# Three layer normalizations whose scaling moves from VectorE to ScalarE, with additions and small matmuls in another order

## The chip, the cores and the metric

One core of one Trainium2 chip runs the whole program in one launch. The metric is the device time of that launch in microseconds (us), median of three runs. The core has five engines with instruction queues of their own: TensorE (PE in the profile, its weight loads PEld), VectorE (DVE), ScalarE (ACT), GpSimd (POOL) and SyncE (SP), which issues the DMAs. They meet only at semaphores.

## The reference

A chain of four blocks over x of shape (2, 1024, 128) in float32, each with a layer normalization in front and a residual addition behind:

```
x = x + attention(norm(x))      # 16 heads of 8, decay by distance
x = x + experts160(norm(x))     # 160 experts of 64, top 8 by sigmoid scores, one shared expert
x = x + memory(norm(x))         # fast-weight memory, chunks of 64 tokens, one after the other
x = x + experts8(norm(x))       # 8 experts of 256, top 2 within groups
norm(x) = (x - mean(x)) / sqrt(var(x) + 1e-5)      # over the 128 features
```

## The kernel before

The 2048 tokens are 16 tiles of 128 tokens on the partitions, in four groups of four tiles (`G` = 4, `TPG` = 4); one group is 512 columns, `GW`, one bank of PSUM. `x` and `xn` hold tokens by features, `xnT` holds features by tokens. The program is written by hand, engine by engine: the order on each engine is the order of its code, and `wait_ge` on counting semaphores ties the engines together. No scheduler moves anything. Each `norm(k)` stands on four engines, k being 0 to 3 for the four blocks:

- VectorE (L1674): for each group `make_x(g)`, the residual addition, then four `bn_stats` (L1686) and four `bn_aggr` (L1689) into `mv` (mean and variance), which raise `var_ready`; one group later four `tensor_scalar` (L1698), (x - mean) * rstd into `xn`, which raise `xn_ready`.
- GpSimd (L680): variance + EPS (L685), then the power -0.5 (L686) into `rstd`, which raises `rstd_ready`.
- TensorE (L1165): four transposes of `xn` into bank 0 or 1 (L1175), which raise `xnT_psum`; then, one group behind, `read_group`, the first products that read `xnT`. For k = 3 four spare matmuls a group (`spares`, L1172) stand ahead of the transposes of groups 1 to 3; their results are written over. Spare matmuls stand elsewhere too (`spare`, L1185); they compute nothing.
- ScalarE (L869): copies the bank into `xnT` (L874), which raises `xnT_ready`, then, one group behind, `follow`.

Around the three later ones:

- `norm(1)` stands behind the attention. `make_x` is the addition of the projection (L1792). `read_group` is `tokens_of`: the shared expert's product (L1307), four router products into PSUM (L1292), and the biases of a later group (L1286). `follow` is `take_group`: two copies for the shared expert (L1015, L1016), the sigmoid of the scores (L1009) and xh, the rounded high part of `xnT` (L882). VectorE then picks the top eight per token, and the chosen weights go through DRAM into the expert loop (L1464, L1471, L1477 on TensorE).
- `norm(2)` stands behind that loop. `make_x` adds the experts' sum (L1957), `read_group` is `token_scalars` (two spares, then L1533), `follow` is `token_gates`, a sigmoid (L887) whose function table has to be loaded first. Behind it come 32 products for half sums (L1523) and the memory's 16 steps. GpSimd has memsets and casts (L832 to L836) ahead of its part and the inverse norms (L842 to L845) behind.
- `norm(3)` stands behind the memory. Four additions of the memory's output (L2046) come first, then all the statistics. 18 spares (L1593) fill TensorE's time. `read_group` is `router_logits2`: four products of eight columns (L1589). `follow` is `high_x`, xh again (L882); GpSimd makes the low part xl (L856). Behind it the first gate and up products of the second expert stage (L1464 by the helper `three`) take xh and xl, while VectorE chooses experts from the logits (L2058 to L2094).

Of the kernel before, what the change touches and what calls it, by code (L numbers as in the profile page):

```python
# [26 lines left out]
P = 128  # L27
# [57 lines left out]
def build(nc, a, out):  # L85
    with ExitStack() as ctx:
# [26 lines left out]
        ident = sb("ident", [P, P])  # L113
        half = sb("half", [P, NT])
# [542 lines left out]
        def _(pool):  # L657
# [22 lines left out]
            def norm(k):  # L680

                for g in range(G):
                    ts = slice(g * TPG, (g + 1) * TPG)
                    pool.wait_ge(var_ready, G * k + g + 1)
                    link(pool.tensor_scalar(rstd[:, ts], mv[:, ts, 1], EPS, None, ALU.add))  # L685
                    pool.tensor_tensor(rstd[:, ts], rstd[:, ts], half[:, ts], ALU.pow).then_inc(rstd_ready, 1)  # L686
# [172 lines left out]
        def _(act):  # L859
# [9 lines left out]
            def norm(k, follow):  # L869
                for g in range(G):  # L870
                    n = G * k + g
                    act.wait_ge(xnT_psum, n + 1)
                    cols = slice(g * GW, (g + 1) * GW)
                    act.activation(xnT[:, cols], bank(n % 2), ACT.Copy).then_inc(xnT_ready, 1)  # L874
                    if g:
                        follow(g - 1)
# [285 lines left out]
        def _(pe):  # L1162
            pe.wait_ge(consts, 1)

            def norm(k, read_group=None, spares=0):  # L1165

                for g in range(G):
                    n = G * k + g
                    if g >= 2:
                        pe.wait_ge(xnT_ready, n - 1)  # L1170
                    for _ in range(spares if g else 0):
                        pe.matmul(bank(n % 2), hh[0][:, 0:P], hh[0][:], start=True, stop=True)  # L1172
                    pe.wait_ge(xn_ready, n + 1)
                    for t in range(TPG):
                        ins = pe.transpose(bank(n % 2)[:, t * P:(t + 1) * P], xn[:, g * TPG + t, :], ident[:])  # L1175
                    ins.then_inc(xnT_psum, 1)
                    if read_group and g:
                        read_group(g - 1)
                if read_group:
                    read_group(G - 1)  # L1180
# [413 lines left out]
            norm(3, router_logits2, 4)  # L1594
# [76 lines left out]
        def _(dve):  # L1671
            link = Link(dve, dve_link)

            def norm(k, make_x=None):  # L1674

                for g in range(G + 1):
# [17 lines left out]
                    if g >= 1:  # L1694
                        tiles = range((g - 1) * TPG, g * TPG)
                        dve.wait_ge(rstd_ready, G * k + g)
# [346 lines left out]
            for g in range(G):  # L2043
# [5 lines left out]

            norm(3)  # L2050
# [114 lines left out]
```

## Time and profile before

| what | us |
|---|---|
| median of three runs | 1058.62 |
| lowest and highest of them | 1057.59, 1058.99 |
| the profiled execution, its own time | 1059.15 |
| its span in the trace | 1057.4 |
| TensorE busy | 1008.4 (95%) |
| VectorE busy | 816.8 (77%) |
| ScalarE busy | 795.7 (75%) |
| GpSimd busy | 233.0 (22%) |

The span runs from the first to the last instruction in the trace, and the time of the run has a little more around it. Busy TensorE includes the spare matmuls. The mean granted clock of TensorE over the span is 0.987 of full speed.

### The profile page before, as it was taken

Reading aid. Unit: us, or ns where it says so; the run is one execution under the profiler, and the core shown is the slowest. Engines: PE = TensorE matmul, PEld = TensorE weight load, DVE = VectorE, ACT = ScalarE, POOL = GpSimd, SP = SyncE. Lnnn points to the kernel's source line nnn. Section 1 sums busy time; section 2 is a strip of 40 time slices with the busy share of each in tenths; the row PEclk is TensorE's granted clock in tenths of the full one; section 3 lists DMA queues with packets and bytes.
Section 4 is the critical chain, followed back from the end, with each engine's and each line's share of the span. In section 5 each row is a group of like instructions: output and inputs, shape, how many; then the busy total and the mean of one; then the engine's idle time right before and its main releaser. Section 6 shows DMA issues by size and latency. Waiting matters only on the chain.

```text
span 1057.4 us, 20303 instructions
## 1 busy us (share of the span) xinstructions
PE 1008.4 (95%) x5242; PEld 684.2 (65%) x5274; DVE 816.8 (77%) x1861; ACT 795.7 (75%) x1331; POOL 233.0 (22%) x359
## 2 busy tenths in 40 slices
PE   5799999999998999999999999999998998999997
PEld 3333333333335688888888888888875887888885
DVE  8644444444449799999999999999996888699997
ACT  5799999999985778788787878778773553655554
POOL 3777765554463000000000000000005112200000
PEclk9799999999999999999999999999999999899999
DMA  4477876777761587677776777777631000034321
GB/s 134 143 230 242 255 250 219 235 225 226 225 202 36 180 309 246 240 243 235 240 241 241 246 245 236 235 245 242 237 98 60 1 2 1 1 128 125 106 102 40
DMA packets 102991, 188.98 MB, mean 179 GB/s; under 512 B 11932, under 2 KB 56604, under 8 KB 102940
## 3 DMA queue, kind: packets, MB, share of 16 engines
q1 hardware_dynamic: 102756, 188.19, 54.8%
q8 instruction: 18, 0.29, 0.1%
q10 hardware_dynamic: 192, 0.30, 0.1%
q14 instruction: 25, 0.20, 0.1%
HBM read 152.46 MB, written 35.98 MB: 178 GB/s over the span
## 4 chain that ended last, share of the span: by engine, by line
PE 86%; DVE 5%; ACT 3%; DMA 2%; issue 2%; POOL 1%; SPq 1%; DVEq 0%; ACTq 0%; POOLq 0%
PE bank L1464 28%; PE bank L1477 16%; PE bank L1362 12%; PE bank L1471 8%; PE bank L1343 6%; PE bank L1346 5%; PE bank L1562 1%; PE bank L1373 1%; DVE xn L1698 1%; PE bank L1185 1%; DVE stats L1686 1%; DVE state L2036 1%; DMA c_rows<-fold 1%; PE bank L1572 1%; PE bank L1292 1%
## 5 line engine op out<-in xcount | busy, mean ns | idle before, releaser
L1464 PE MATMUL bank<-xh,w_parts 128*128 128x512 f32 x896 | 277.4, 391 | 0.9 <-DVEq L1936 0.9
L969 ACT ACTIVATE ring<-bank,minus_bound 128x1024 f32<-128x1024 f32 x256 | 263.0, 1118 | 13.8 <-PE bank L1346 8.8
L1069 ACT ACTIVATE bank<-bank 128x512 f32<-128x512 f32 x320 | 186.2, 582 | 88.7 <-PE bank L1464 88.7
L1950 DVE TENSOR_TENSOR bank<-bank,ring 128x512 f32<-128x512 f32 x320 | 223.8, 699 | 25.2 <-DMA ring<-c_rows 2.8
L1477 PE MATMUL bank<-hh,w_parts 128*128 128x512 f32 x772 | 237.9, 389 | 0.0
L1942 DVE TENSOR_TENSOR hl<-bank,hh 128x512 fp32r<-128x512 f32 x321 | 218.4, 680 | 0.1
L1842 DVE TENSOR_TENSOR bank<-bank,corner 128x128 f32<-128x128 f32 x256 | 76.4, 298 | 154.3 <-PE bank L1346 151.2
L1464 PEld LDWEIGHTS bank<-xh,w_parts 128*128 128x128 f32 x896 | 168.0, 189 | 37.5 <-DVEq L1936 1.7
L1063 ACT ACTIVATE hh<-bank 128x512 fp32r<-128x512 f32 x321 | 190.4, 593 | 0.8 <-DVE bank L1950 0.5
L1464 PE MATMUL bank<-xl,w_parts 128*128 128x512 f32 x448 | 174.8, 390 | 0.0
L1477 PEld LDWEIGHTS bank<-hh,w_parts 128*128 128x128 f32 x772 | 144.8, 188 | 30.6 <-ACT hh L1063 0.8
L1471 PE MATMUL bank<-hl,w_parts 128*128 128x512 f32 x387 | 151.8, 392 | 2.5 <-DVE hl L1942 2.3
L1362 PE MATMUL bank<-ring,v_cur 128*32 128x512 f32 x1024 | 137.6, 610 | 0.1
L1343 PEld LDWEIGHTS bank<-q_stack,k_stack 128*128 128x128 bf16 x320 | 30.5, 98 | 115.8 <-ACT ring L969 96.3
L832 POOL MEMSET q_stack<- 128x512 f32 x2 | 1.0, 530 | 466.2 <-PE bank L1471 466.2
L1343 PE MATMUL bank<-q_stack,k_stack 128*128 128x384 bf16 (+2 forms) x320 | 97.7, 322 | 1.8 <-issue 0.2
L1346 PE MATMUL bank<-q_stack,k_stack 128*128 128x512 bf16 (+3 forms) x352 | 94.0, 327 | 4.2 <-DMA k_stack<-k_parts 4.2
L1464 PEld LDWEIGHTS bank<-xl,w_parts 128*128 128x128 f32 x448 | 84.4, 188 | 17.8
L1471 PEld LDWEIGHTS bank<-hl,w_parts 128*128 128x128 f32 x387 | 72.6, 188 | 22.3 <-DVE hl L1942 6.1
L1146 ACT ACTIVATE q_stack<-bank 128x512 f32<-128x512 f32 x58 | 34.7, 598 | 51.7 <-PE bank L1464 49.8
L2111 DVE TENSOR_TENSOR q_stack<-big,ring 128x512 f32<-128x512 f32 x64 | 44.3, 693 | 11.4 <-ACTq L1126 3.0
L1362 PEld LDWEIGHTS bank<-ring,v_cur 128*32 128x32 f32 x1024 | 20.2, 108 | 48.6 <-ACT ring L969 39.9
(320 smaller groups left out, 1137.7 us busy)
## 6 DMA issues: line engine op xcount, KB each, us to landing
ring<-c_rows SPq DMA_DIRECT2D x173, 512.0 KB, 4.7
w_parts<-w_pairs SPq DMA_DIRECT2D x160, 128.0 KB, 2.9
w_pairs<-xh SPq DMA_DIRECT2D x16, 768.0 KB, 4.3
q_stack<-q_parts SPq DMA_DIRECT2D x63, 144.0 KB
k_stack<-k_parts SPq DMA_DIRECT2D x189, 48.0 KB
w_pairs<-xl SPq DMA_DIRECT2D x16, 512.0 KB, 3.0
big<-in_w_exp SPq DMA_DIRECT2D x16, 384.0 KB, 4.8
w_ffn_parts<-xl SPq DMA_DIRECT2D x16, 384.0 KB, 3.7
```

The source lines that it names most:

```text
L969: act.activation(ring[:, c % RING * S:(c % RING + 1) * S], wide[(m + c) % SB][:], ACT.Exp, bias=minus_bound[:]).then_inc(exp_done, 1)
L1063: act.activation(hh[(c - 1) % 2][:], hidden, ACT.Copy).then_inc(split, 1)
L1069: act.activation(bank(4 + c % ZB), bank(4 + c % ZB), ACT.Silu).then_inc(silu_ready, 1)
L1343: ins = pe.matmul(wide[(m + c) % SB][:, lo:mid], k_stack[0][u][:, keys], q_stack[1][u][:, lo:mid], start=True, stop=True)
L1346: ins = pe.matmul(wide[(m + c) % SB][:, mid:hi], k_stack[1][u][:, keys], q_stack[0][u][:, mid:hi], start=True, stop=True)
L1362: ins = pe.matmul(bank(6 + u)[at:at + 32, :], v_cur[u][:, done_step % QT, :], ring[:, at_ring + h * 512:at_ring + (h + 1) * 512], start=(d ...
L1464: ins = pe.matmul(out_, w[i], x_[j], start=start and k == 0, stop=stop and k == 2, skip_group_check=not start)
L1471: return pe.matmul(bank(done_step % G), w[0], hl[done_step % 2][:], start=False, stop=False, skip_group_check=True)
L1477: ins = pe.matmul(bank(done_step % G), part, hh[done_step % 2][:], start=opens and k == 0, stop=False, skip_group_check=True)
L1842: dve.tensor_tensor(tile, tile, corner[:], ALU.mult).then_inc(corner_done, 1)
L1942: dve.tensor_tensor(hl[(c - 1) % 2][:], hidden, hh[(c - 1) % 2][:].bitcast(F32), ALU.subtract).then_inc(split, 1)
L1950: dve.tensor_tensor(bank(4 + c % ZB), bank(4 + c % ZB), cb[u][:, g * GW:(g + 1) * GW], ALU.mult).then_inc(hid_ready, 1)
```

## The change

Normalization 0 stays as it is. In 1, 2 and 3:

- VectorE no longer scales; its `norm` ends with the statistics of the last group.
- GpSimd makes a second column per tile, `shift` = -mean * rstd: a negation of the mean ahead of the addition of EPS, a product behind the power. `rstd_ready` is raised behind the product.
- ScalarE makes `xn` = rstd * x + shift, four activations of 128x128 a group with the function Identity and both columns as operands. In its queue xn of group g stands ahead of the copy of xnT of group g-1, and `follow` of group g-2 behind that.

In 3 alone the addition of the memory's output stands ahead of the statistics of its own group instead of all four ahead, the logits of a group stand behind its own transposes instead of behind the next group's, and two spares a group (in bank 7, groups 0 to 3) stand between the two, where there were four ahead of the transposes of groups 1 to 3.

```diff
@@ GpSimd
+                    if k:
+                        link.sign(pool.tensor_scalar(shift[:, ts], mv[:, ts, 0], -1.0, None, ALU.mult))
                     link(pool.tensor_scalar(rstd[:, ts], mv[:, ts, 1], EPS, None, ALU.add))
-                    pool.tensor_tensor(rstd[:, ts], rstd[:, ts], half[:, ts], ALU.pow).then_inc(rstd_ready, 1)
+                    ins = pool.tensor_tensor(rstd[:, ts], rstd[:, ts], half[:, ts], ALU.pow)
+                    if k:
+                        link(ins)
+                        ins = pool.tensor_tensor(shift[:, ts], shift[:, ts], rstd[:, ts], ALU.mult)
+                    ins.then_inc(rstd_ready, 1)
@@ ScalarE
             def norm(k, follow):
-                for g in range(G):
-                    n = G * k + g
-                    act.wait_ge(xnT_psum, n + 1)
-                    cols = slice(g * GW, (g + 1) * GW)
-                    act.activation(xnT[:, cols], bank(n % 2), ACT.Copy).then_inc(xnT_ready, 1)
-                    if g:
-                        follow(g - 1)
+                for g in range(G + 1):
+                    if g < G:
+                        act.wait_ge(rstd_ready, G * k + g + 1)
+                        for t in range(g * TPG, (g + 1) * TPG):
+                            ins = act.activation(xn[:, t, :], x[:, t, :], ACT.Identity, bias=shift[:, t:t + 1], scale=rstd[:, t:t + 1])
+                        ins.then_inc(xn_ready, 1)
+                    if g >= 1:
+                        n = G * k + g - 1
+                        act.wait_ge(xnT_psum, n + 1)
+                        cols = slice((g - 1) * GW, g * GW)
+                        act.activation(xnT[:, cols], bank(n % 2), ACT.Copy).then_inc(xnT_ready, 1)
+                    if g >= 2:
+                        follow(g - 2)
@@ TensorE
-                    for _ in range(spares if g else 0):
-                        pe.matmul(bank(n % 2), hh[0][:, 0:P], hh[0][:], start=True, stop=True)
                     pe.wait_ge(xn_ready, n + 1)
...
-                    if read_group and g:
+                    if spares:
+                        for _ in range(spares):
+                            pe.matmul(bank(7), hh[0][:, 0:P], hh[0][:], start=True, stop=True)
+                        read_group(g)
+                    elif read_group and g:
                         read_group(g - 1)
-                if read_group:
+                if read_group and not spares:
                     read_group(G - 1)
...
-            norm(3, router_logits2, 4)
+            norm(3, router_logits2, 2)
@@ VectorE
-                for g in range(G + 1):
+                for g in range(G if k else G + 1):
...
-                    if g >= 1:
+                    if g >= 1 and k == 0:
                         tiles = range((g - 1) * TPG, g * TPG)
-                        dve.wait_ge(rstd_ready, G * k + g)
+                        dve.wait_ge(rstd_ready, g)
...
-            for g in range(G):
+            def add_memory(g):
...
-            norm(3)
+            norm(3, add_memory)
```

ScalarE in normalization 2, from the last copies of the expert stage on. `xnT` is the transposed input, `big` the rows of token scalars. Before:

```order
L1081 ACTIVATE state<-bank 128x128 x2
L874 ACTIVATE xnT<-bank 128x512 x2
L887 ACT_TABLE_LOAD
L887 ACTIVATE big<-bank,b_pair 2x512
L874 ACTIVATE xnT<-bank 128x512
L887 ACTIVATE big<-bank,b_pair 2x512
L874 ACTIVATE xnT<-bank 128x512
L887 ACTIVATE big<-bank,b_pair 2x512 x2
```

And of the change:

```order
L1094 ACTIVATE state<-bank 128x128 x2
L881 ACTIVATE xn<-x,shift,rstd 128x128 x8
L887 ACTIVATE xnT<-bank 128x512
L881 ACTIVATE xn<-x,shift,rstd 128x128 x4
L887 ACTIVATE xnT<-bank 128x512
L900 ACT_TABLE_LOAD
L900 ACTIVATE big<-bank,b_pair 2x512
L881 ACTIVATE xn<-x,shift,rstd 128x128 x4
L887 ACTIVATE xnT<-bank 128x512
L900 ACTIVATE big<-bank,b_pair 2x512
L887 ACTIVATE xnT<-bank 128x512
L900 ACTIVATE big<-bank,b_pair 2x512 x2
```

Two groups of scaling stand ahead of the first copy of xnT, the third ahead of the second copy, and the fourth behind the table load and the first sigmoid.

TensorE in normalization 3, from the 18 spares to the first gate product; `hh` are the spares, `w_gate` the logits. Before:

```order
L1185 MATMUL bank<-xh 128x512 x18
L1175 MATMUL bank<-ident,xn 128x128 x4
L1172 MATMUL bank<-hh 128x512 x4
L1175 MATMUL bank<-ident,xn 128x128 x4
L1589 MATMUL bank<-w_gate,xnT 128x8 x4
L1172 MATMUL bank<-hh 128x512 x4
L1175 MATMUL bank<-ident,xn 128x128 x4
L1589 MATMUL bank<-w_gate,xnT 128x8 x4
L1172 MATMUL bank<-hh 128x512 x4
L1175 MATMUL bank<-ident,xn 128x128 x4
L1589 MATMUL bank<-w_gate,xnT 128x8 x8
L1464 MATMUL bank<-xh,w_parts 128x512 x2
```

And of the change, the first two of four equal groups and what follows the fourth's transposes:

```order
L1200 MATMUL bank<-xh 128x512 x18
L1186 MATMUL bank<-ident,xn 128x128 x4
L1190 MATMUL bank<-hh 128x512 x2
L1604 MATMUL bank<-w_gate,xnT 128x8 x4
L1186 MATMUL bank<-ident,xn 128x128 x4
L1190 MATMUL bank<-hh 128x512 x2
L1604 MATMUL bank<-w_gate,xnT 128x8 x4
...
L1190 MATMUL bank<-hh 128x512 x2
L1604 MATMUL bank<-w_gate,xnT 128x8 x4
L1479 MATMUL bank<-xh,w_parts 128x512 x2
```

The logits of a group moved from behind the next group's transposes to behind their own; of the last eight together four remain, and of 12 spares eight.

VectorE at the start of normalization 3. Before:

```order
L2046 TENSOR_TENSOR x<-x,bank 128x512 x4
L1686 BN_STATS stats<-x 128x6 x4
L1689 BN_AGGR mv<-stats 128x2 x4
L1686 BN_STATS stats<-x 128x6 x4
L1689 BN_AGGR mv<-stats 128x2 x4
L1698 TENSOR_SCALAR xn<-x,mv,rstd 128x128 x4
```

And of the change:

```order
L2062 TENSOR_TENSOR x<-x,bank 128x512
L1701 BN_STATS stats<-x 128x6 x4
L1704 BN_AGGR mv<-stats 128x2 x4
L2062 TENSOR_TENSOR x<-x,bank 128x512
L1701 BN_STATS stats<-x 128x6 x4
L1704 BN_AGGR mv<-stats 128x2 x4
```

One addition now stands ahead of each group's statistics, and the scaling is gone from the queue.

## Rows read from the trace of the kernel before

**Rows 1.** The page, part 4: shares of the chain that ended last, by engine.
```profile
PE 86%; DVE 5%; ACT 3%; DMA 2%; issue 2%; POOL 1%; SPq 1%; DVEq 0%; ACTq 0%; POOLq 0%
```

**Rows 2.** Chain of waits in normalization 1: start us, us, what.
```profile
326.87 1.43 PE bank L1307 x2
...
330.77 0.71 ACT big L1009
...
334.85 0.71 ACT big L1009
```

**Rows 3.** Chain of waits in normalization 2.
```profile
811.91 0.59 PE bank L1175 x4
...
814.78 3.64 PE bank L1523 x32
```

**Rows 4.** Chain of waits in normalization 3 and behind it.
```profile
903.82 0.84 PE bank L1175 x4
904.65 3.21 PE bank L1589 x16
907.87 9.87 PE bank L1464 x36
917.74 0.45 PE bank L1185 x2
```

**Rows 5.** Timeline of VectorE (DVE), normalizations 2 and 3: start us, us, line, operation.
```profile
798.46 0.69 DVE L1957 TENSOR_TENSOR x<-x,bank 128x512 f32<-128x512 f32 x1 [4.96 <-PE bank L1509]
...
800.43 0.69 DVE L1957 TENSOR_TENSOR x<-x,bank 128x512 f32<-128x512 f32 x1
...
802.61 1.11 DVE L1698 TENSOR_SCALAR xn<-x,mv,rstd 128x128 f32<-128x128 f32 x4 [0.17 <-POOL rstd L686]
...
889.31 2.48 DVE L2046 TENSOR_TENSOR x<-x,bank 128x512 f32<-128x512 f32 x4 [0.81 <-PE bank L1580]
...
900.75 3.01 DVE L1698 TENSOR_SCALAR xn<-x,mv,rstd 128x128 f32<-128x128 f32 x4 [0.54 <-POOL rstd L686]
...
916.22 0.29 DVE L2094 TENSOR_TENSOR combine<-combine,r_sum 128x128 f32<-128x128 f32 x1
```

**Rows 6.** Timeline of GpSimd (POOL), normalizations 1, 2 and 3.
```profile
320.56 0.23 POOL L685 TENSOR_SCALAR rstd<-mv 128x4 f32<-128x4 f32 x1 [0.64 <-DVE mv L1689]
...
801.16 0.23 POOL L685 TENSOR_SCALAR rstd<-mv 128x4 f32<-128x4 f32 x1 [0.20 <-POOL hl L836]
801.47 1.04 POOL L686 TENSOR_TENSOR rstd<-rstd,half 128x4 f32<-128x4 f32 x1
...
902.15 1.27 POOL L856 TENSOR_TENSOR xl<-xnT,xh 128x512 fp32r<-128x512 f32 x1 [0.26 <-ACT xh L882]
```

**Rows 7.** Busy time in stretches of 2 us: PE, PEld, DVE, ACT, POOL, PEclk, DMA, GB/s.
```profile
804.00:806.00 2.00, 0.44 (x4) 0.20 (x2) 1.93 (x11) 0.60 (x1) 0.27 (x1) 1.00 0.01 3
...
902.00:904.00 2.00, 0.91 (x6) 0.45 (x5) 1.76 (x3) 0.07 (x1) 1.27 (x1) 1.00 0.00 0
...
906.00:908.00 2.00, 2.00 (x10) 2.00 (x11) 0.03 (x1) 1.11 (x1) 1.15 (x1) 0.50 0.00 0
```

**Rows 8.** Groups of ScalarE (ACT) by shape: count | busy us, mean ns | idle before.
```profile
L882 ACT ACTIVATE xh<-xnT 128x512 fp32r<-128x512 f32 x8 | 5.0, 621 | 0.0
...
L1043 ACT ACTIVATE ring<-ring,top_inv 128x160 f32<-128x160 f32 x12 | 4.0, 414 | 0.0
...
L1078 ACT ACTIVATE vg_cat<-vg2T 128x128 f32<-128x128 f32 x1 | 0.3, 312 | 1.2 <-PE bank L1515 1.2
```

**Rows 9.** Timeline of ScalarE: behind normalization 1, in 2, behind 3.
```profile
342.33 2.65 ACT L1043 ACTIVATE ring<-ring,top_inv 128x160 f32<-128x160 f32 x8
...
808.09 1.28 ACT L887 ACT_TABLE_LOAD   x1
809.39 0.68 ACT L887 ACTIVATE big<-bank,b_pair 2x512 f32<-2x512 f32 x1
...
911.26 0.59 ACT L1117 ACTIVATE xn<-bank 128x512 f32<-128x512 f32 x1
```

More of the change, by code:

```diff
@@ L113, in build @@
         ident = sb("ident", [P, P])
+        shift = sb("shift", [P, NT])
         half = sb("half", [P, NT])
```

## The prediction

> **What bounds the kernel now.** I read the page first, then the chain of waits, then the three stretches where a normalization stands between two large stages. TensorE holds 86% of the chain, VectorE 5%, ScalarE 3% [rows 1]: the loops are TensorE's, and the change doesn't touch them. It touches three joints: normalization 1 (318 to 331 us, before the router), 2 (798 to 815, before the memory stage) and 3 (889 to 908, before the second expert stage). Outside them every instruction keeps its place, so what a joint gains or loses should pass through whole. In each the chain runs over VectorE's statistics and its scaling of xn, GpSimd's power, the transposes, and then TensorE's readers. The reader should look at when the first instruction of the next stage starts: the first `shared` product at 326.87 [rows 2], the half sums at 814.78 [rows 3], the first gate product at 907.87 [rows 4].
>
> In joint 3 two things stand out. VectorE's four additions come first, 2.48 us together, before any statistics, and the last group of four scalings took 3.01 us where an ordinary one takes 1.11 [rows 5]: in those 3 us GpSimd was making xl, 1.27 us apiece [rows 6]. And TensorE's clock fell: granted 1.00 in 902 to 904, where TensorE was busy 0.91 of 2 us, and 0.50 (1.2 of 2.4 GHz) in 906 to 908 although it was busy throughout [rows 7]. The last 16 logits products (3.21 us, eight columns wide each) and the first gate products ran at that clock [rows 4].
>
> **The change part by part.**
>
> *VectorE loses the scaling.* A group of addition, statistics, aggregate and scaling is now a group of the first three, 1.97 us (800.43 minus 798.46, where the scaling does not stand between) [rows 5]. The 12 groups of scaling, 1.11 us each, leave VectorE.
>
> *GpSimd's step grows.* Before, a group was 0.31 (start of the addition of EPS to the start of the power, 801.16 to 801.47) and 1.04 for the power [rows 6]. Now a negation stands ahead and a product behind, both of 128x4. The trace has neither; the nearest row is the 128x4 tensor_scalar, 0.23. I take 0.2 for the first (it waits for nothing) and 0.07 + 0.23 for the second. A group is 0.2 + 0.31 + 1.04 + 0.07 + 0.23 = 1.85 us, just under VectorE's 1.97, so GpSimd keeps pace but every result comes 0.5 us later after its statistics.
>
> *ScalarE gains the scaling.* Four 128x128 activations with a scale and a bias that are both columns. The trace has none with both. Plain: 312 ns at 128 columns and 621 at 512, 0.80 ns a column; with a scale column: 414 at 160 columns, where the plain line gives 338 [rows 8]. So one column operand costs 76 ns. A second one costs between nothing (388 ns) and as much again (464 ns). I take 464, since nothing shows the two reads to be shared. Eight in a row took 2.65 us [rows 9], a pitch of (2.65 - 0.41)/7 = 0.32, so 0.09 of each is overlapped. A group is 3 x 0.37 + 0.46 = 1.57 us; with a free second column 1.27. VectorE took 1.11.
>
> The Trainium skill has a rule here that speaks against the move (ScalarE: Activation LUTs, section What ACT_TABLE_LOAD costs): each pointer operand adds about 93 ns and successive activations overlap by about the same. By it a group would be some 1.64 us, an estimate, and the sum below 0.3 us worse. The row at 160 columns agrees with it for one operand within 0.02 us; no run here yet shows two.
>
> Identity as the function is new. In the order ScalarE has seven table loads before and seven after, at the same neighbours, so I cost it at nothing.
>
> *Joint 1: -0.3.* GpSimd starts at 320.56 [rows 6]; rstd of group 0 is there at 322.4, of group 1 at 324.25, of group 2 at 326.1. ScalarE scales group 1 from 324.35 to 325.9 and copies xnT(0), which now stands behind that, to 326.5. The first shared product starts at 326.6 instead of 326.87 [rows 2]. From there the rhythm is 334.85 - 330.77 = 4.08 us a group [rows 2], set by TensorE and the copy of the gates. ScalarE's own share of such a period, each less the overlap of 0.09, is now xh 0.5, xn(3) 1.5, xnT 0.5, two shared copies 1.0 and the gates 0.6, 4.1 us: it just fits in the one period where xn(3) stands, and is free later.
>
> *Joint 2: +0.8.* GpSimd starts at 801.16, late because of its memsets [rows 6]. Results come at 803.0, 804.9, 806.7. ScalarE: xn(0) to 804.65, xn(1) 805.0 to 806.55, xnT(0) to 807.1, xn(2) to 808.6, xnT(1) to 809.2. Then comes, ahead of xn(3), what the old order had beside VectorE's work: the sigmoid's table load, 1.28, and the first sigmoid, 0.68 [rows 9], to 811.1. xn(3) ends at 812.65 and the last transposes start at 812.7, where they started at 811.91 [rows 3]. Queued behind the load are xn(3) and xnT(2); who waits is TensorE. With the cheap activation it would be 811.9, so nothing lost.
>
> *Joint 3: -2.2.* Each addition now stands ahead of its own group's statistics, and TensorE waits for xnT of a group right behind that group's transposes and two spares. The first addition starts at 889.31 [rows 5]. Statistics are there at 891.3 and each 1.97 later; GpSimd's results at 893.35, 895.3, 897.3, 899.3. ScalarE: xn(0) 893.4 to 895.0, xn(1) 895.35 to 896.9, xnT(0) to 897.45; xn(2) 897.4 to 898.95, xnT(1) to 899.5, xh(0) to 900.0, xn(3) to 901.5, xnT(2) to 902.05. TensorE: logits(0) 897.5 to 898.3 (half of 3.21/2, at the full clock), then tp(1), logits(1) 899.6 to 900.4, tp(2) to 901.05, logits(2) to 902.9, tp(3) to 903.55; xnT(3) to 904.15, logits(3) to 905.0. The two spares a group (0.23 each [rows 4]) fit into the wait for xnT. So the first gate product could start at 905.0 against 907.87: -2.9. ScalarE's queue and its round trip with TensorE set the pace here, no longer VectorE.
>
> But half the spares are gone. Per group of some 2.6 us TensorE has 0.6 of transposes [rows 3], 0.5 of spares and 0.8 of logits, and the rows say that the logits don't hold the clock up: it stayed at 0.50 while only they ran [rows 4, 7]. I expect a fall inside this joint, about a group earlier than before, which doubles one logits group and one set of transposes: +1.1, leaving -1.8. Then it should be up again for the gate products, whose 36 took 9.87 with the first at half clock [rows 4]; at full clock they are 36 x 0.23 = 8.2, but the thirteenth waits until ScalarE has emptied the first pair of banks, at 911.85 [rows 9], 4.0 after the first; with 24 x 0.23 behind that it is 9.5: -0.4. VectorE's routing ended at 916.5 [rows 5], 1.3 before the products at 917.74 [rows 4], and moves along, so it stays hidden.
>
> *Sum.* -0.3 + 0.8 - 2.2 = -1.7 us. The profiled execution took 1059.15 (span 1057.4), so it would be 1057.45; the median of the three timed runs is 1058.62, 0.5 lower, and on that scale I forecast **1056.9 us**.
>
> **The rivals.**
> - *No fall of the clock in joint 3* (1055.8). For it: in 804 to 806 TensorE was busy only 0.44 of 2 us and the clock held at 1.00 [rows 7]. Then joint 3 gives -2.9 - 0.4, the sum is -2.8.
> - *The second column operand is free* (1055.2). Joint 1 gives -0.6, joint 2 nothing, joint 3 another -0.6: -3.4. Against it: the first one cost 76 ns.
> - *The clock falls late and stays down into the gate products, as before* (1057.8): joint 3 -1.3, the sum -0.8. For it: that is what the trace shows already, with more spares.
> - *Slower: the clock falls in joint 2* (1060.2). TensorE now has nothing from about 810.5 to 812.7, where ScalarE loads its table, with the 32 half sums (3.64 us [rows 3]) behind. A fall there puts some 6.6 us of work at half rate, as in joint 3 before, +3.3, so the sum is +1.6. It decides if that gap is judged worse than the thin stretch 804 to 806 that passed [rows 7]. A small further part is that the scaling group is over 2 us, when ScalarE paces all three joints.
>
> **How the numbers follow.** Forecast case 0.42 (own range 1056.0 to 1057.8), no fall 0.20, free operand 0.12, late fall 0.18, slower rival 0.08. About 0.2%, 2.1 us, is what a measurement of this kernel can tell from no change, so "faster" means below 1056.5. The first rival and the second lie there nearly whole (0.30) and the edge of the forecast case adds 0.08: 0.38. Slower needs over 1060.7, the upper half of its rival: 0.05. The rest is 0.57. The range runs from the free operand, 1055.0, past the late fall to the lower part of the slower rival, 1059.3.
>
> **What would show it, and what would make it wrong.** Right: xn by ScalarE, about 460 ns apiece; GpSimd 1.85 a group; the last transposes of joint 2 some 0.8 later against its first addition; from the first addition of joint 3 to the first gate product 15.7 to 16.8 us instead of 18.56; a granted clock of 0.50 in the midst of joint 3 and 1.00 in the gate products. Wrong: activations near 390 or over 500 ns, a table load ahead of an xn, a fall of the clock in joint 2, or a loop whose rhythm changed.

## The result, and the profile after

| what | before | after |
|---|---|---|
| median, us | 1058.32 (20 runs) | 1061.11 (20 runs) |
| lowest and highest, us | 1053.09, 1061.79 | 1057.96, 1065.52 |
| ratio, 95% interval | | 1.0033 [1.0021, 1.0044] |
| profiled execution, us (span) | 1059.15 (1057.4) | 1060.83 (1058.9) |
| mean granted clock, profiled execution | 0.987 | 0.985 |
| VectorE, ScalarE, GpSimd busy, us | 816.8, 795.7, 233.0 | 801.9, 813.5, 237.2 |

The change makes the kernel slower by about 3.5 us by the ratio (0.0033 x 1058; the two medians lie 2.8 us apart). The forecast was 1056.9 with a range up to 1059.3, so it was wrong in size and in sign. The work did move as described: VectorE lost 14.9 us of busy time, ScalarE gained 17.8.

The page of the changed kernel, parts 1 and 4: busy us of each engine, and the shares of the chain that ended last.

```profile
PE 1011.2 (95%) x5270; PEld 683.6 (65%) x5270; DVE 801.9 (76%) x1813; ACT 813.5 (77%) x1379; POOL 237.2 (22%) x383
...
PE 86%; ACT 4%; DVE 3%; DMA 2%; POOL 2%; issue 1%; SPq 1%; DVEq 0%; ACTq 0%; POOLq 0%
```

VectorE's two points of the chain [rows 1] are now ScalarE's and GpSimd's. TensorE's share didn't shrink.

Single traces have to be compared with care: of the 1.5 us between the two spans 1.0 had arisen ahead of joint 1 (its first addition starts at 319.09, against 318.07), where nothing was changed. Over all traces of this case that start lies between 315.1 and 319.1, so joints are measured from their own first instruction.

**The new operations.** All ScalarE scalings together (count, shortest, median and longest in ns), then GpSimd's timeline in normalization 3 (start us, us, line, operation).

```profile
L881 ACT ACTIVATE xn<-x,shift,rstd x48: 477/478/496, 323.6 to 902.6; 128x128 f32<-128x128 f32 x48
```
```profile
892.71 0.23 POOL L687 TENSOR_SCALAR shift<-mv 128x4 f32<-128x4 f32 x1 [5.46 <-DVE mv L1704]
893.02 0.23 POOL L688 TENSOR_SCALAR rstd<-mv 128x4 f32<-128x4 f32 x1
893.33 1.04 POOL L689 TENSOR_TENSOR rstd<-rstd,half 128x4 f32<-128x4 f32 x1
894.45 0.20 POOL L692 TENSOR_TENSOR shift<-shift,rstd 128x4 f32<-128x4 f32 x1
894.73 0.24 POOL L687 TENSOR_SCALAR shift<-mv 128x4 f32<-128x4 f32 x1
```

A scaling takes 478 ns, where 464 was expected. GpSimd starts a group every 2.02 us (892.71 to 894.73), where 1.85 was expected and VectorE needs 1.97: GpSimd is now the slower of the two, by a little.

**Joint 2.** Chain of waits of the changed kernel: start us, us, what.

```profile
805.35 1.65 ACT xn L881 x4
806.99 0.48 ACT xnT L887
807.47 1.54 ACT xn L881 x4
809.01 0.48 ACT xnT L887
...
809.51 1.28 ACT L900
810.79 0.01 issue
810.80 0.68 ACT big L900
811.48 1.55 ACT xn L881 x4
...
813.17 0.63 PE bank L1186 x4
...
816.07 3.64 PE bank L1538 x32
```

This is the queue that the prediction wrote down: table load (1.28), first sigmoid (0.68), only then the last scaling, and TensorE's last transposes behind it. From GpSimd's first memset there to the half sums it is 18.66 us, against 17.57 before.

**Joint 3.** Chain of waits of the changed kernel, then its windows of 2 us with the columns of [rows 7] (PEclk is the last but two). The first gate product was at 907.87 before [rows 4].

```profile
890.61 0.70 DVE x L2062
...
896.71 1.65 ACT xn L881 x4
898.36 0.49 ACT xnT L887
...
898.89 1.06 PE bank L1604 x8
...
901.12 1.06 PE bank L1604 x8
...
903.93 1.71 PE bank L1604 x8
...
907.44 1.71 PE bank L1604 x8
909.15 9.89 PE bank L1479 x36
```
```profile
897.00:899.00 2.00, 0.69 (x4) 0.25 (x4) 1.48 (x9) 2.00 (x6) 1.69 (x4) 1.00 0.00 0
899.00:901.00 2.00, 1.90 (x14) 1.47 (x14) 0.00 (x0) 1.90 (x6) 1.47 (x4) 1.00 0.02 4
901.00:903.00 2.00, 1.88 (x13) 1.88 (x14) 0.00 (x0) 2.00 (x6) 1.27 (x1) 0.78 0.00 0
903.00:905.00 2.00, 2.00 (x9) 1.45 (x8) 0.00 (x0) 1.23 (x3) 0.69 (x1) 0.50 0.00 0
...
907.00:909.00 2.00, 2.00 (x10) 1.73 (x9) 0.00 (x0) 1.98 (x3) 1.18 (x1) 0.50 0.00 0
```

The first logits come 8.28 us after the first addition (898.89 - 890.61); the prediction had 8.2. Then the clock falls and stays at 0.50. A group of logits takes 1.71 instead of 1.06, and from one group to the next it is 3.51 us (907.44 - 903.93) instead of 2.23 (901.12 - 898.89). First addition to first gate product: 18.54 us, against 18.56 before. What the new order won up to there went to the clock.

**Joint 1.** The first gates come 11.50 us after the first addition, against 12.70 before, and the expert loop's first product (at 354.02, before at 355.09) after 34.93 against 37.02. But a later step of that loop waits for routing rows that go out to DRAM and come back. Chain of the changed kernel, then of the kernel before:

```profile
354.78 6.94 DMA c_rows<-fold
361.73 4.33 DMA ring<-c_rows
```
```profile
355.96 5.79 DMA c_rows<-fold
361.76 4.22 DMA ring<-c_rows
```

By the clock of the trace both writes land at 361.7, but joint 1 began 1.02 us later in the changed kernel. From the joint's first addition the write starts after 35.69 us, against 37.89, and lands after 42.63, against 43.68; the rows are back after 46.97, against 47.91. So more than half of the 2.2 us won at the write's start went into a longer write, and 0.9 was left in this pair. It doesn't hold over more traces: where the chain takes this path, the write lands 42.6 to 44.7 us after the first addition with the changed joint 1 (seven traces) and 41.9 to 45.4 with the old one (six).

### The profile page after: what moved, and what is told of

It reads as the page before. It is cut to its first block, busy times and chain, and to the rows that moved or that the text cites. A ratio compares the mean times of both kernels' runs of the same rounds, so it can differ in the third digit from the quotient of the medians.

```text
span 1058.9 us, 20341 instructions
## 1 busy us (share of the span) xinstructions
PE 1011.2 (95%) x5270; PEld 683.6 (65%) x5270; DVE 801.9 (76%) x1813; ACT 813.5 (77%) x1379; POOL 237.2 (22%) x383
## 4 chain that ended last, share of the span: by engine, by line
PE 86%; ACT 4%; DVE 3%; DMA 2%; POOL 2%; issue 1%; SPq 1%; DVEq 0%; ACTq 0%; POOLq 0%
PE bank L1479 28%; PE bank L1492 16%; PE bank L1377 12%; PE bank L1486 8%; PE bank L1361 6%; PE bank L1358 6%; PE bank L1577 1%; PE bank L1388 1%; ACT xn L881 1%; PE bank L1200 1%; DMA c_rows<-fold 1%; DVE state L2051 1%; POOL rstd L689 1%; PE bank L1587 1%; DMA k_stack<-k_parts 1%
## 5 line engine op out<-in xcount | busy, mean ns | idle before, releaser
L1965 DVE TENSOR_TENSOR bank<-bank,ring 128x512 f32<-128x512 f32 x320 | 223.9, 700 | 26.4 <-DMA ring<-c_rows 4.4
L1361 PE MATMUL bank<-q_stack,k_stack 128*128 128x512 bf16 (+3 forms) x384 | 99.8, 333 | 3.8 <-DMA k_stack<-k_parts 3.8
L1479 PEld LDWEIGHTS bank<-xl,w_parts 128*128 128x128 f32 x448 | 84.5, 189 | 17.8
```

The lines of the kernel that those rows point to most:

```text
L1361: ins = pe.matmul(wide[(m + c) % SB][:, mid:hi], k_stack[1][u][:, keys], q_stack[0][u][:, mid:hi], start=True, stop=True)
L1479: ins = pe.matmul(out_, w[i], x_[j], start=start and k == 0, stop=stop and k == 2, skip_group_check=not start)
L1965: dve.tensor_tensor(bank(4 + c % ZB), bank(4 + c % ZB), cb[u][:, g * GW:(g + 1) * GW], ALU.mult).then_inc(hid_ready, 1)
```

## The experiments

The letters of the theories are those of the expectations. The joints are measured in each trace in the same way: joint 2 from GpSimd's first memset to the first half sum, joint 3 from the first addition of the memory's output to the first gate product, both by the starts in the timelines. Such a start lies some 0.15 us ahead of the chain's, which cuts off what overlaps: the 18.56 and 18.54 above are 18.41 and 18.39 in this measure. "Mean clock" is the granted clock of the span, averaged over all timed executions of a kernel (10 to 12 of each, 7 of one, 150 of the kernel before). Over the executions of one and the same kernel the time rises by 0.67 us for each 0.001 that this clock is lower (one slope fitted to all of them), which goes with the several us between single runs.

**One joint at a time**, and the table load moved. In the first three the other two joints are as before:

```diff
@@ joint1_only (in the same way: joint2_only, joint3_only)
-                    if k:
+                    if k == 1:
@@ all_table_early: the whole change, and ahead of normalization 2 in ScalarE's queue
+            act.activation(early_table[:], half[:, 0:1], ACT.Sigmoid)
```

> Only normalization 1 is scaled by ScalarE; normalizations 2 and 3 stand as before. In the profile of the change joint 1 took 47.1 us from its first addition to the loop's first product with the chosen weights, against 48.0 before. Theory A (each joint's change passes through whole, the loss is joint 2's): 0 to -1 us against before. Rival (the change's loss is spread, ScalarE's queue costs in every joint): +1 us.

> Only normalization 2 is scaled by ScalarE. Theory A: the table load and the first sigmoid ahead of the last group of scaling make joint 2 longer by 1.1 us (18.8 against 17.7 us from the first memset of GpSimd to the half sums), so +1 to +1.5 us against before. Rival (spread loss, or chance of the clock): within 0.5 us of before.

> Only normalization 3 is changed, with its additions between the statistics, logits behind own transposes and two spares a group. Theory A: TensorE's clock falls inside the joint and eats what the scaling gained; 18.5 us from the first addition to the first gate product as before, 0 to +1 us against before, a granted clock of 0.50 in more than 8 us of it. Rival: the clock's fall there was one execution's accident, the joint takes 16 us and the run is 2 us faster than before.

> The whole change, and one tiny sigmoid of ScalarE ahead of normalization 2, so that its table is loaded before the scaling and not between the third and the fourth group. Theory A: the last transposes of joint 2 start 1.3 us earlier than in the change, joint 2 takes 17.5 us, and the run is 1.2 us faster than the change. Rival (something else sets joint 2, for one the clock that fell from 806.8 to 810.2): less than 0.4 us faster than the change.

| kernel | ratio to before, 95% | joint 2 | joint 3 | mean clock |
|---|---|---|---|---|
| joint1_only | 1.0002 [0.9984, 1.0020] | 17.91 | 16.77 | 0.9890 |
| joint2_only | 1.0011 [0.9991, 1.0030] | 18.72 | 16.76 | 0.9882 |
| joint3_only | 1.0018 [1.0001, 1.0034] | 18.10 | 19.26 | 0.9836 |
| all_table_early | 1.0028 [1.0007, 1.0050] | 18.17 | 19.26 | 0.9835 |

Joint 1 shows nothing, with an interval from -1.7 to +2.1 us. Joint 2 costs about 1.2 us by its ratio, though the interval takes in zero, and joint 3 1.9 (0 to 1 was expected). The three together are 3.3 us, about the whole loss. The early table gave 0.5 us (1.0028 against 1.0033), between its two forecasts and within the noise. A surprise is in the column of joint 3: the old one takes 16.8 us in two traces, not the 18.41 of the profile on which the prediction stood. Windows of joint1_only:

```profile
899.00:901.00 2.00, 0.93 (x5) 0.45 (x4) 1.85 (x4) 0.16 (x1) 1.27 (x1) 1.00 0.00 0
901.00:903.00 2.00, 2.00 (x19) 2.00 (x19) 0.00 (x0) 1.39 (x3) 0.21 (x1) 1.00 0.00 0
```

The same code, with the same gap in TensorE's work, kept 1.00 here and fell to 0.50 in the profile of before [rows 7]. In joint2_only it fell as well, but only behind the first gate product (0.50 from 905.4 to 908.7).

**Joint 3 taken apart.**

```diff
@@ joint3_five_spares: joints 1 and 2 as before
-            norm(3, router_logits2, 2)
+            norm(3, router_logits2, 5)
@@ joint3_scale_only: only the scaling of normalization 3 on ScalarE, order and spares as before
@@ joint3_order_only: VectorE scales; additions, logits and spares in the change's order
@@ joint3_additions_only: only this
-            for g in range(G): add_memory(g)
-            norm(3)
+            norm(3, add_memory)
```

> Normalization 3 alone is changed as in the change, but with five spares a group between transposes and logits instead of two. Theory A (two spares let TensorE's clock fall, and the logits can't bring it back): the granted clock stays at 1.00 through the joint, from the first addition to the first gate product it takes 15.7 to 16.5 us instead of 19.3 in joint3_only, and the run is 2 to 3 us faster than that one, 0.5 to 1 us faster than before. Rival (the fall comes from the wait for ScalarE between transposes and logits, whatever fills it, or the spares delay the logits): 18 us or more.

> Only the scaling of normalization 3 goes to ScalarE; the four additions stand ahead of all statistics and the logits behind the next group's transposes with four spares, as before. Theory A (the order and the spares are what loses, not the scaling): 16 to 17 us for the joint with the clock at 1.00. Rival (ScalarE's 1.6 us a group is the loss): 18 us or more at a full clock.

> VectorE scales as before in all normalizations; in 3 the additions stand between the statistics, and the logits behind own transposes with two spares. Theory A: the clock falls in the joint as in joint3_only, 0.50 for more than 6 us, and the joint takes 18.5 to 20 us. Rival: without ScalarE's longer groups the gaps are short enough and it takes under 17 us.

> Everything as before but the four additions of the memory, each ahead of its own group's statistics. Theory A: VectorE sets the joint, its group is then 3.0 us (addition, statistics, scaling) and the last scaling of the joint ends at most 0.3 us from where it did, since VectorE's work is the same; the first transposes start 1.8 us earlier. The joint takes 16.5 to 18.5 us, by the clock. Rival: the earlier start passes through whole, 15 us.

| kernel | ratio to before, 95% | joint 3 | mean clock |
|---|---|---|---|
| joint3_five_spares | 0.9985 [0.9973, 0.9998] | 16.51 | 0.9908 |
| joint3_scale_only | 1.0003 [0.9990, 1.0017] | 16.44 | 0.9899 |
| joint3_order_only | 1.0019 [1.0002, 1.0036] | 18.23 | 0.9835 |
| joint3_additions_only | 1.0006 [0.9986, 1.0026] | 18.15 | 0.9896 |

The two kernels with the change's order and two spares, with the scaling (joint3_only) and without it (joint3_order_only), have the same ratio and the same low clock, though joint3_order_only, at 18.23, is a little shorter than the 18.5 to 20 expected. So the scaling on ScalarE is not what costs here; the order with its few spares is. In the trace of joint3_additions_only the clock fell too, but came back inside the joint, where the old order has its spares. Its windows:

```profile
899.00:901.00 2.00, 2.00 (x7) 1.81 (x8) 0.68 (x3) 0.47 (x1) 1.28 (x1) 0.50 0.00 0
901.00:903.00 2.00, 2.00 (x12) 1.70 (x11) 0.00 (x0) 0.38 (x1) 0.00 (x0) 0.59 0.00 0
903.00:905.00 2.00, 2.00 (x17) 1.87 (x17) 0.50 (x2) 1.98 (x3) 1.19 (x1) 1.00 0.00 0
```

**The whole change with more spares**, the change itself again beside it, and the kernel before with more spares.

```diff
@@ change_again: nothing
@@ all_five_spares (two_joints_five_spares: normalization 2 as before as well)
-            norm(3, router_logits2, 2)
+            norm(3, router_logits2, 5)
@@ before_seven_spares: the kernel before
-            norm(3, router_logits2, 4)
+            norm(3, router_logits2, 7)
```

> The changed kernel once more, beside the next three on one chip, so that they can be set against it directly. Theory A (the loss stands in joint 2, +1.1 us, and in a joint 3 where TensorE's granted clock falls to 0.50): joint 2 again 18.7 us from GpSimd's first memset to the half sums, joint 3 18.4 to 19.3 us with 0.50 for most of 901 to 911, ratio 1.001 to 1.004. Theory B (the loss is the chance of single executions, mostly the start of the program): ratio 0.999 to 1.001, joint 3 as short as 16.8 us.

> The whole change, with five spares a group in normalization 3 in place of two, nothing else. Theory A: the spares keep the granted clock at 1.00 through joint 3, which takes 16.5 us from the first addition to the first gate product instead of 18.4 to 19.3; joint 2 keeps its 18.7. The time is 1.9 to 2.8 us below the changed kernel's beside it, that is a ratio to the kernel before of 0.999 to 1.001. Theory C (the order alone brought the gain of joint_3_five_spares, and the clock is no cause): joint 3 stays at 18 us or more and the time is the changed kernel's.

> Normalization 2 as before, 1 and 3 as in the change, with five spares a group in 3. Theory A: joint 3 at 16.5 us, joint 2 at 17.6 to 18.1 instead of 18.7, joint 1 worth nothing since the wait for the routing rows takes up its gain: 0.7 us below all_five_spares, ratio 0.9980 to 0.9995, and no better than joint_3_five_spares's 0.9985. Theory D (joint 1 does bring its 0.3 to 1.2 us): ratio 0.997 to 0.998, clearly better than that.

> The kernel before with seven spares ahead of the transposes of groups 1 to 3 of normalization 3 in place of four, nothing else. Theory A, strong form (all that can be won here is the clock): the granted clock stays at 1.00 in 898 to 910, joint 3 takes 16.8 us in every execution instead of 16.8 in some and 18.4 in others, ratio 0.9985 to 0.9998, as good as joint_3_five_spares. Theory E (the spares lengthen TensorE's queue there: nine more of 0.21 us, of which 0.6 us a group stands ahead of transposes that VectorE's scaling has already released): joint 3 17.5 to 18.7 us, ratio 0.9998 to 1.001.

| kernel | median, us | ratio to before, 95% | joint 2 | joint 3 | mean clock |
|---|---|---|---|---|---|
| change_again | 1060.56 | 1.0033 [1.0014, 1.0051] | 18.66 | 19.87 | 0.9842 |
| all_five_spares | 1058.20 | 1.0009 [0.9988, 1.0030] | 18.67 | 16.53 | 0.9900 |
| two_joints_five_spares | 1056.51 | 0.9989 [0.9970, 1.0008] | 19.29 | 16.52 | 0.9902 |
| before_seven_spares | 1058.15 | 0.9999 [0.9980, 1.0019] | 18.10 | 16.83 | 0.9903 |

Three spares more a group, twelve products that compute nothing, take 2.4 us off the change's median. In the trace joint 3 is 3.3 us shorter. Chain and windows of all_five_spares there:

```profile
898.11 1.17 PE bank L1209 x5
899.27 0.79 PE bank L1623 x8
900.06 0.49 PE bank L1205 x4
900.55 1.17 PE bank L1209 x5
901.72 0.79 PE bank L1623 x8
```
```profile
897.00:899.00 2.00, 2.00 (x15) 1.82 (x15) 0.00 (x0) 1.91 (x5) 1.24 (x2) 1.00 0.01 4
...
901.00:903.00 2.00, 2.00 (x17) 1.86 (x16) 0.00 (x0) 0.79 (x2) 1.13 (x1) 1.00 0.00 0
```

A group is now 2.45 us (901.72 - 899.27), all of it TensorE's own work at full clock: spares 1.17, logits 0.79, transposes 0.49.

Theory B (chance of single executions) and C (the order brought the gain) fall: joint 3 is 19.87 us in change_again, and 16.53 with the same order and more spares. The two ratios' intervals overlap, but the mean clocks lie apart, 0.9842 and 0.9900. Theory E falls in its price, 16.83 against 17.5 to 18.7. The strong form of A (0.9985 to 0.9998) is not shown: seven spares in the old order gained nothing measurable (0.9999), and the interval takes in both forecasts. The old order's mean clock is 0.9893 over all its executions, and there was little to win back.

Two_joints_five_spares lies in theory A's range (0.9989), and its interval reaches into D's, so it doesn't decide between them; its joint 2, the old one, took 19.29 and not 17.6 to 18.1, with the clock at 0.50 there from 805 to 812.

**Gap or narrow products?** TensorE stands idle 1.31 us ahead of the first logits of the change, and its logits products are only eight columns wide, each with a weight load of 128x128 (one for each, in the trace's count). The next two fill one or the other.

```diff
@@ five_in_first_group, the whole change (five_in_later_groups: (2, 5, 5, 5))
-                        for _ in range(spares):
+                        for _ in range((5, 2, 2, 2)[g]):
@@ all_three_spares
-            norm(3, router_logits2, 2)
+            norm(3, router_logits2, 3)
@@ all_five_table_early: all_five_spares with the small sigmoid of all_table_early
```

> The change with five spares in group 0 of normalization 3 and two in groups 1 to 3. Theory F (the fall begins in TensorE's gap between the first transposes and the first logits, and later the clock is only held where it is): the granted clock stays at 1.00 through joint 3, 16.5 to 17.0 us, mean clock over the executions 0.990. Theory N (the narrow logits products let the clock fall whatever stands ahead of them, and it takes spares in every group): the clock falls to 0.50 one or two groups later, joint 3 17.3 to 18.5 us, mean clock 0.985 to 0.988.

> The change with two spares in group 0 of normalization 3 and five in groups 1 to 3. Theory F: the gap ahead of the first logits is as in the change, 1.3 us, so the clock falls at 897 to 901, and five full-width spares a group may or may not bring it back before the gate products; joint 3 17.5 to 19.5 us, mean clock 0.984 to 0.987. Theory N: the later groups are now dense with full-width products and the clock stays at 1.00 or is back after one group, joint 3 16.5 to 17.2 us, mean clock 0.989 to 0.990.

> The change with three spares a group in normalization 3 instead of two. If the clock answers to the spares as a step that lies between two and five, this tells on which side three stand: at 1.00 throughout and joint 3 at about 16.5 us (mean clock 0.990), or at 0.50 for about 10 us and joint 3 at 18.4 to 20 us plus 1.3 us for three more spares at half clock (mean clock 0.983 to 0.985). Theory N makes something between likely, a fall in some executions and a return within the joint.

> The whole change, with five spares a group in normalization 3 and a small sigmoid ahead of normalization 2 in ScalarE's queue, which loads the table there. Theory A: joint 3 at 16.5 us and joint 2 at 18.2 instead of 18.7 us; 0.5 us below all_five_spares, ratio to the kernel before 0.999 to 1.001, so the whole change with both repairs is about even with the kernel before and not better. If the table's place were all that costs in joint 2, it would be at 17.4 us and the ratio 0.998 to 0.9995.

| kernel | ratio to before, 95% | joint 2 | joint 3 | mean clock (lowest, highest) |
|---|---|---|---|---|
| five_in_first_group | 1.0029 [1.0001, 1.0057] | 18.67 | 16.21 | 0.9874 (0.980, 0.994) |
| five_in_later_groups | 1.0018 [1.0000, 1.0035] | 18.67 | 16.51 | 0.9897 (0.985, 0.993) |
| all_three_spares | 1.0033 [1.0016, 1.0050] | 19.36 | 19.68 | 0.9850 (0.983, 0.987) |
| all_five_table_early | 1.0010 [0.9994, 1.0025] | 17.26 | 16.53 | 0.9904 (0.986, 0.994) |

With the later groups filled and the gap as in the change, the clock held. TensorE's timeline of five_in_later_groups (the gap stands in brackets) and one of its windows:

```profile
897.78 1.06 PE L1624 MATMUL bank<-w_gate,xnT 128*128 128x8 f32 x8 [1.31 <-ACT xnT L902]
898.69 0.63 PE L1206 MATMUL bank<-ident,xn 128*128 128x128 f32 x4
899.08 1.40 PE L1210 MATMUL bank<-hh 128*128 128x512 f32 x5
```
```profile
901.00:903.00 2.00, 2.00 (x15) 1.76 (x15) 0.00 (x0) 2.00 (x5) 0.83 (x1) 1.00 0.00 0
```

With the gap filled and the later groups thin, the fall was not gone but moved; windows of five_in_first_group:

```profile
905.00:907.00 2.00, 1.78 (x15) 1.34 (x14) 0.00 (x0) 1.23 (x3) 1.04 (x2) 1.00 0.00 0
907.00:909.00 2.00, 2.00 (x9) 1.71 (x9) 1.24 (x4) 1.92 (x3) 1.21 (x1) 0.57 0.00 0
```

It came in the gate products, where it cost next to nothing in this trace (the 36 took 9.90 us, against 9.82 in all_five_spares at 1.00). Over its ten executions the mean clock is spread from 0.980 to 0.994, from the change's lowest (0.980) nearly to the highest of all_five_spares (0.995).

Theory F falls in its first half: the gap alone doesn't bring the fall. In its second half it is open: this trace kept 1.00 up to the gate products, as F had it, and only the mean clock (0.9874, where F had 0.990) speaks against it. Theory N holds in its outline, that the later groups need the spares. All_three_spares stands with the change (0.9850), all_five_spares doesn't (0.9900). It has twelve spares in joint 3, as many as the kernel before, so it is not their number alone: in the new order it took more of them. Whether that is the place of the logits or the place of the spares no run here tells apart. What the chip looks at isn't known from this, only how these orders came out. The ratio of five_in_later_groups (1.0018) is above that of all_five_spares (1.0009), within both intervals.

In joint 2 the early table takes 18.67 down to 17.26 where the clock held (all_five_table_early), and to 18.17 where it fell to 0.50 in 809 to 811 (all_table_early). Its chain:

```profile
807.69 0.48 ACT xnT L901
808.18 0.57 ACT big L914
808.74 1.54 ACT xn L895 x4
810.29 0.14 issue
810.42 0.63 PE bank L1205 x4
```

No table load stands ahead of the last scaling, so the load's place was the whole of joint 2's loss in that trace, against the 0.5 us that theory A gave it. In the time it doesn't show against all_five_spares (1.0010 and 1.0009, with intervals 3.3 and 4.4 us wide).

**Is any version faster?** Only joint3_five_spares had an interval below one, so it was run again, unchanged.

> The kernel with only normalization 3 as in the change and five spares a group, once more, to see whether its gain holds beside another set of runs. If it is real: ratio to the kernel before 0.997 to 0.9995, joint 3 at 16.5 us with the granted clock at 1.00 throughout, mean clock 0.990 to 0.991. If the first measurement was luck: ratio 0.9995 to 1.001.

It measured 1056.38 us, ratio 0.9998 [0.9983, 1.0013], with joint 3 at 16.53 and a mean clock of 0.9904. The joint is as short as before, but the gain of 1.6 us did not come again, though the two intervals overlap. No version is shown to beat the kernel before; what is shown is that this one is not slower by more than 0.13%.

## Why the prediction was wrong

**Joint 3, predicted -2.2, is the step that failed.** It measured 0.0 in the profiled pair (18.56 to 18.54), and +1.9 us by the ratio of joint3_only. The first logits came within 0.1 us of their time. Three things were wrong in the step.
- *"a fall inside this joint ... which doubles one logits group and one set of transposes"*. The fall was forecast, its length was not. It lasted from 902 to 912 in the profile of after, over the last two groups of logits and the first gate products, and from 897 on over three groups in joint3_only. The evidence was in the prediction itself: "it stayed at 0.50 while only they ran". The step should have taken that row at its word and priced every group behind the fall: 3.51 - 2.23 = 1.28 us each.
- *"Then it should be up again for the gate products"*, -0.4. It wasn't: 36 of them took 9.89 us, as before (9.87). But the term was wrong in itself. In joint1_only, at 1.00 throughout, they took 9.84 from the first to the spares behind them. There TensorE waits 1.28 us ahead of the thirteenth (its timeline stands below) for ScalarE, which loads a table (1.28 us) before it empties the banks. In the chain of before no such wait stands; the slow products fill that time. A full clock in the first gate products is worth some 0.03 us and not 0.4. Only a fall that lasts further costs there: 10.19 to 10.84 us in joint3_only, all_table_early, all_three_spares and joint3_order_only.
- *The kernel before was taken as one trace shows it.* That trace had a fall in joint 3 that its other executions often don't have (16.8 us in two other traces of the same code). The -2.2 was reckoned from that long joint. From 16.8 even an undisturbed new order wins only 0.6 (16.21), and a disturbed one loses 1.6 to 3.1 (18.4 to 19.9).

TensorE's timeline of joint1_only at the thirteenth gate product (start us, us, line, operation, in brackets the idle time ahead and what ended it):

```profile
907.44 0.70 PE L1498 MATMUL bank<-xh,w_parts 128*128 128x512 f32 x2 [1.28 <-ACT xn L1146]
```

The forecast of 15.7 us for an undisturbed clock measured 16.21 in five_in_first_group (16.36 by the chain, in which the forecast was reckoned). Less than 0.1 of the difference lies ahead of the first logits. The rest stands behind them, where a group's logits took 1.06 us in that trace (I had 0.8).

**Joint 2, predicted +0.8**, was right in mechanism, and the chain shows it piece by piece. It measured +1.1 in the profiled pair, and as much wherever the clock held in joint 2 (17.57 and 17.60 against 18.67 and 18.72). Over the traces the old joint 2 takes 17.57 to 19.29 with a median of 18.1 (ten traces), the changed one 18.66 to 19.36 with a median of 18.67 (seven): +0.6. A fall of the clock lengthens the old joint 2 (to 18.1) and mostly not the changed one, whose chain then runs over ScalarE.

**Joint 1, predicted -0.3**, gave nothing that can be measured; 0.3 is far inside the interval of joint1_only. The gates came 1.2 us sooner in the profiled pair, but only because the clock had fallen there before (0.50 from 327 to 331); in the one trace of the old joint 1 at full clock (joint3_additions_only) they come 11.12 us after the first addition, against 11.50 to 11.52 in four traces of the changed one, so the change is 0.4 later. Behind them a longer write of the routing rows (6.6 to 7.1 us in seven traces, 5.4 to 6.8 in six of the old joint) takes up what is won. The step stopped at the router's rhythm and didn't follow the chain on to the DMA at 355.

**Durations.** The scaling, 464 against 478 ns, was near. The second column operand is not free. The Trainium skill (ScalarE: Activation LUTs, What ACT_TABLE_LOAD costs) gives 186 ns plus 93 for each pointer plus 0.833 a column, an estimate of 479, and the trace agrees at 478. GpSimd's 1.85 was 2.02: I gave the negation 0.2 where its pitch is 0.31, as of any such operation in that queue.

**The rivals.** "The clock falls late and stays down into the gate products" was the nearest in kind, but at 1057.8 its price lacked the comparison with an undisturbed joint. The slower rival put the decisive fall in joint 2. The clock did fall there (0.50 from 807 to 810 in the profile of after, as in eight of the ten traces of the old joint 2), but the chain ran over ScalarE meanwhile, and it was back at 1.00 ahead of the half sums, 3.64 us as before [rows 3]. The right mechanism stood in the wrong joint. That the changed kernel did come out slower doesn't support that rival. Slower had 5% of the chance because the old kernel was taken to lose as much to the clock as the new one.

**How much is the clock?** The change's mean clock is 0.0051 below that of before (0.9842, 0.9893). By the slope of 0.67 us for 0.001 that is 3.4 us of the 3.5. The rest are small terms of both signs: joint 2's wait, and joint 3's shorter order. That share is a fit over executions, not a part taken out and measured, and it is likely too large, since half clock costs nothing where TensorE would wait anyway, as in the first gate products. The measured part is the 2.4 us that all_five_spares gives back. The traces agree with it: joint 3 and the 36 gate products together take 28.3 to 29.7 us, on average 29.2, in four traces with the change's joint 3 (0.50 for 10 to 14 us of it), 28.3, 26.6 and 26.7 in three with the old one (7, 0 and 3 us), and 26.4 in each of the six with five spares in the later groups.

## What to carry to other kernels

A spare matmul stands in an order for a reason: before taking any out, or moving the work around them, look whether the trace shows the clock at half while only the products beside them run, and price all that follows at that clock, up to the next place where the engine would wait anyway. Keeping their number was not enough here: twelve in the new order let the clock fall, twelve in the old order mostly not. Take a joint's length from several executions before reckoning a gain against it, since a granted clock of 0.50 in one trace can be chance and in another order the rule. Ahead of moving work onto an engine's queue, look for a table load that the other engine's work used to run beside, and follow each gain to the next wait for another engine or a DMA.

## What the runs showed of the hardware

- TensorE can be busy all of the time and stay at half clock. In the trace of the change it was busy 2.00 of 2 us in each window from 903 to 909 at a granted 0.50, on transposes, two full-width spares and eight-column logits a group. The Trainium skill (TensorE: Matmul & The Clock Gate, Part 1: The HAM clock gate) says that the gate follows how busy the engine has been. Taken by the profile's busy time, that would have this stretch back at full clock and joint 3 shorter by up to 1.9 us, an estimate (1.28 for the group from 903.93 and 0.65 for the logits at 907.44, 1.71 against 1.06). The trace doesn't agree, and the measurement decides.
- With five spares in each of the later groups the clock was at 1.00 through joint 3 in all six traces, with two in every group in none of five. With the joint 3 of before it was at 1.00 up to the first gate product in two of three, and in one of these two it fell right behind it.
- Half the clock cost next to nothing where TensorE had a wait for ScalarE to fill: the 36 gate products took 9.84 us at 1.00 (joint1_only), with 1.28 us of waiting, and 9.89 in the change, at 0.50 over the first 3 us of them.
- The power of -0.5 on 128x4 takes GpSimd 1.04 us, the 128x4 operations around it 0.20 to 0.23, and the issue between the four is 0.3 us of a group's 2.02.
